# First attention's projections as unrounded half products of 64 stationary columns, in place of three rounded terms

## What is computed

```
x = x + xattn0(queries: context, keys and values: LN(x) and context)
x = x + top-1 of 8 experts, hidden width 512, silu(a) * g
x = x + xattn1(queries: LN(x), 16 heads of 8, keys and values: context)
x = x + top-2 of 8 experts, hidden width 256
```

## Time and profile before

| what | value |
|---|---|
| median of 3 runs | 791.95 us (790.49 to 792.25) |
| span of the profiled execution | 788.3 us |
| what lies between the two | 3.65 us |
| TensorE busy | 706.3 us, 90% |
| its weight loads | 430.8 us, 55% |
| VectorE busy | 475.7 us, 60% |
| ScalarE busy | 378.0 us, 48% |
| GpSimd busy | 377.4 us, 48% |

### The profile page before, as it was taken

One profiled execution on the slowest core, in us unless ns is written; L12 is line 12 of the kernel. 1 busy time (PEld: TensorE's weight loads), 2 busy tenths in 40 slices (PEclk: granted clock), 3 DMA queues, 4 the chain that ended last, 5 costly groups with the idle time before them and its releaser, 6 DMA issues.

```text
span 788.3 us, 13872 instructions
## 1 busy us (share of the span) xinstructions
PE 706.3 (90%) x4810; PEld 430.8 (55%) x4810; DVE 475.7 (60%) x966; ACT 378.0 (48%) x580; POOL 377.4 (48%) x361
## 2 busy tenths in 40 slices
PE   4899999999999999999999999997995687568991
PEld 3654555545556555556545545566995343336661
DVE  4745484585585875667477478465443386845553
ACT  4475554564654554655445444344552643223440
POOL 7264453473464475444464553634333304674552
PEclk9999999999999999999999999998998697569996
DMA  9999999990000000000030004301212500122325
GB/s 253 197 201 197 204 190 10 4 4 1 1 1 2 1 14 1 1 1 1 1 121 2 1 1 108 114 24 32 72 32 80 155 1 28 35 75 69 88 66 177
DMA packets 109867, 50.62 MB, mean 64 GB/s; under 512 B 44804, under 2 KB 103048, under 8 KB 109800
## 3 DMA queue, kind: packets, MB, share of 16 engines
q1 hardware_dynamic: 106280, 42.46, 36.0%
q0 software_dynamic: 3520, 7.27, 2.7%
HBM read 20.07 MB, written 29.64 MB: 63 GB/s over the span
## 4 chain that ended last, share of the span: by engine, by line
PE 74%; DVE 11%; issue 5%; ACT 3%; POOL 3%; DMA 2%; another core or an unknown queue 1%; SPq 1%; DVEq 0%; POOLq 0%; ACTq 0%
PE PSUM L1631 14%; PE PSUM L1663 13%; PE PSUM L1598 5%; PE PSUM L1463 5%; PE PSUM L1498 4%; PE PSUM L1468 4%; PE PSUM L1729 4%; PE PSUM L1423 3%; PE PSUM L1425 2%; PE PSUM L1424 2%; PE PSUM L1612 2%; PE PSUM L1605 2%; PE PSUM L1649 2%; PE PSUM L1693 2%; DVE REC L1377 1%
## 5 line engine op out<-in xcount | busy, mean ns | idle before, releaser
L866 ACT ACTIVATE PT<-PSUM 128x1024 f32<-128x1024 f32 x128 | 128.6, 1024 | 134.1 <-PE PSUM L1631 133.7
L690 POOL TENSOR_TENSOR PSUMS<-PT 128x1024 f32<-128x1024 f32 x32 | 76.0, 2376 | 210.4 <-ACT PT L866 171.4
L690 POOL TENSOR_TENSOR PSUMS<-PSUMS,PT 128x1024 f32<-128x1024 f32 x62 | 149.6, 2413 | 16.8 <-ACT PT L866 9.9
L1254 DVE TENSOR_REDUCE TOPS<-PSUM 128x2 f32<-128x1024 f32 x128 | 152.1, 1220 | 6.9 <-PE PSUM L1598 6.5
L1663 PE MATMUL PSUM<-PT,BIG 128*64 128x512 f32 x512 | 130.6, 611 | 0.0
L1209 DVE TENSOR_TENSOR SIL<-SIL,PSUM 128x256 f32<-128x256 f32 (+1 forms) x62 | 32.2, 519 | 65.7 <-ACT SIL L783 46.8
L1244 DVE TENSOR_TENSOR KL<-PSUM,KH 128x512 fp32r<-128x512 f32 x32 | 22.1, 691 | 68.2 <-ACT KH L844 67.7
L1598 PE MATMUL PSUM<-KH,QH 64*128 64x512 f32 x256 | 57.9, 449 | 4.0 <-DVE QL L1247 3.7
L1663 PEld LDWEIGHTS PSUM<-PT,BIG 128*64 128x64 f32 x512 | 28.4, 135 | 53.4 <-issue 52.0
L1598 PEld LDWEIGHTS PSUM<-KH,QH 64*128 64x128 f32 x256 | 24.2, 183 | 59.2 <-DVE TOPS L1254 24.9
L783 ACT ACTIVATE SIL<-PSUM 128x256 f32<-128x256 f32 (+1 forms) x62 | 28.6, 462 | 56.7 <-PE PSUM L1463 31.4
(11 more groups left out here) (256 smaller groups left out, 1365.5 us busy)
## 6 DMA issues: line engine op xcount, KB each, us to landing
lists_d<-EMPTY SPq DMA_DIRECT2D x3, 2730.0 KB, 35.3
lists_b<-EMPTY SPq DMA_DIRECT2D x3, 2470.0 KB, 33.4
lists_d<-EMPTY SPq DMA_DIRECT2D x1, 2665.0 KB, 34.9
XG<-lists_d SPq DMA_DIRECT2D x39, 65.0 KB
lists_b<-EMPTY SPq DMA_DIRECT2D x1, 2405.0 KB, 17.2
BIG<-in_L_ffn_w SPq DMA_DIRECT2D x1, 2048.0 KB
W2ALL<-in_L_ffn_w SPq DMA_DIRECT2D x4, 512.0 KB, 6.2
PT<-results_d SPq DMA_DIRECT2D x8, 256.0 KB, 4.4
```

Of the source, the lines that this page charges most:

```text
L690: pool.tensor_tensor(PSUMS[:, i % 2], PTT[:, i % 2, 0] if kt == 1 else PSUMS[:, i % 2], PTT[:, i % 2, kt], ALU.add).then_inc(s_ps, 1)
L866: act.activation(PTT[:, i % 2, kt], PSUM[:, place:place + 2, :], ACT.Exp, scale=DH ** -0.5).then_inc(s_exp, 1)
L1254: dve.tensor_reduce(TOPS[:, c, 0, :], PSUM[:, place:place + 2, :], AX.X, ALU.max).then_inc(s_max, 1)
```

## The change

A helper `halves` makes a product as two matmuls of 64 stationary columns, onto partitions 0 to 63 and 64 to 127, with the same moving operand. The projections of the first attention use it on unrounded weights and features instead of `three`. The splits of weights, context and features go, with their buffers (WH, WL, XTH, XTL, CTH, CTL) and semaphores; WA gets a place of its own, and VectorE writes the features straight into XF, two deep. The context values are made once. `qk` has a semaphore for the queries and one for the keys. All other unrounded products named above take the same form, except the down products, gate and up of the second experts, attention × values, and the small sums. The loads of the first experts' gate weights are cut differently: experts 3 and 7 come last.

```diff
-            WH = sb1("WH", 3, INNER)
-            WL = sb1("WL", 3, INNER)
-            XTH = sb1("XTH", 2, S)
-            XTL = sb1("XTL", 2, S)
+            WA = sb1("WA", 3, INNER)
+            XF = sb1("XF", 2, S)
...
             sp.wait_ge(s_sc, context_of(2 * B - 1))
-            gates_of(0, E - 1)
+            gates_of(0, GROUP - 1)
+            gates_of(GROUP, E - 1)
             sp.wait_ge(s_sc, len(scored))
+            gates_of(GROUP - 1, GROUP)
             gates_of(E - 1, E)
...
-                    act.wait_ge(ld_w1, 48)
+                    act.wait_ge(ld_w1, 80)
...
-                    act.wait_ge(s_qk, a + 1)
+                    act.wait_ge(s_qp, a + 1)
...
                     act.activation(QH[:, a % 2, :], PSUM[:, place, :], ACT.Copy).then_inc(s_qkh, 1)
+                    act.wait_ge(s_kp, a + 1)
                     act.activation(KH[:, a % 2, :], PSUM[:, place + 1, :], ACT.Copy).then_inc(s_qkh, 1)
...
-                dve.tensor_scalar(XT[:, :], PSUM[:, bank, :], GAINS[:, 0:1], GAINS[:, 1:2], ALU.mult, ALU.add).then_inc(XTD.sem, 1)
-            def split_features(b):
-                k = b % 2
-                dve.wait_ge(s_xth, b + 1)
-                dve.wait_ge(*XTD.at(b, "feat"))
-                dve.tensor_tensor(XTL[:, k, :], XT[:, :], XTH[:, k, :].bitcast(F32), ALU.subtract).then_inc(XTD.sem, 1)
+                if b >= 2:
+                    dve.wait_ge(s_kp, (b - 1) * PAIRS)
+                    dve.wait_ge(s_vp, (b - 1) * KT)
+                dve.tensor_scalar(XF[:, b % 2, :], PSUM[:, bank, :], GAINS[:, 0:1], GAINS[:, 1:2], ALU.mult, ALU.add).then_inc(s_xf, 1)
...
+            def halves(dst, stationary, moving, start=True, stop=True):
+                for n in range(0, P, 64):
+                    last = pe.matmul(dst[n:n + 64], stationary[:, n:n + 64], moving, start=start, stop=stop)
+                return last
...
-                        last = pe.matmul(PSUM[:, bank + n, c:c + P], WS[:, 2 * (g % 2) + n, c:c + P], XGT[:, g % 3, :],
-                                         start=True, stop=True)
+                        last = halves(PSUM[:, bank + n, c:c + P], WS[:, 2 * (g % 2) + n, c:c + P], XGT[:, g % 3, :])
...
                     for n in range(2):
-                        c = slice(n * BANK, (n + 1) * BANK)
-                        last = three(PSUM[:, place + n, :], XTH[:, k, cols], XTL[:, k, cols], WH[:, 2, c], WL[:, 2, c])
+                        last = halves(PSUM[:, place + n, :], XF[:, k, cols], WA[:, 2, n * BANK:(n + 1) * BANK])
...
-                    for w in range(2):
-                        last = three(PSUM[:, place + w, :], WH[:, w, c], WL[:, w, c], XTH[:, k, :], XTL[:, k, :])
-                    last.then_inc(s_qk, 1)
+                    for w, made in enumerate((s_qp, s_kp)):
+                        halves(PSUM[:, place + w, :], WA[:, w, c], XF[:, k, :]).then_inc(made, 1)
...
-                            last = pe.matmul(PSUM[:, place, t * P:(t + 1) * P], OT[:, (GROUP * a + c) % OTS, t * P:(t + 1) * P],
-                                             WOUT[:, (GROUP * a + c) % PAIRS, :], start=c == 0, stop=c == GROUP - 1)
+                            last = halves(PSUM[:, place, t * P:(t + 1) * P], OT[:, (GROUP * a + c) % OTS, t * P:(t + 1) * P],
+                                          WOUT[:, (GROUP * a + c) % PAIRS, :], start=c == 0, stop=c == GROUP - 1)
...
-                            last = pe.matmul(PSUM[:, c, t * P:(t + 1) * P], QT[a][r, t * P:(t + 1) * P], KBD[r, a, :, :],
-                                             start=True, stop=True)
+                            last = halves(PSUM[:, c, t * P:(t + 1) * P], QT[a][r, t * P:(t + 1) * P], KBD[r, a, :, :])
```

More of the change, by code:

```diff
@@ L259, in build @@
         s_tr = sem("lane_turned")
[L260 to L264, removed]
+        CTD = Steps(sem("ctx_dve"), ["ct", "raw"])
+        s_xf = sem("features")
         s_const_r = sem("rounded_consts")
@@ L1537, in context_keys @@
                     c = slice(pr * P, (pr + 1) * P)
-                    last = three(PSUM[:, 7 - part, pr % GROUP * P:(pr % GROUP + 1) * P], WH[:, 1, c], WL[:, 1, c], CTH[:, :], CTL[:, :])
+                    last = halves(PSUM[:, 7 - part, pr % GROUP * P:(pr % GROUP + 1) * P], WA[:, 1, c], CT)
                 last.then_inc(s_kc, 1)
                 free[7 - part] = s_kcf, part + 1
-            pe.wait_ge(s_cth, 1)
-            pe.wait_ge(*CTD.at(0, "low"))
-            pe.wait_ge(s_wl, 1)
+            pe.wait_ge(*CTD.at(0, "ct"))
+            pe.wait_ge(ld_wk, 16)
             context_keys(0)
-            turn_nrm(RUN_OF["a", 0], 6, XTD.at(0, "feat"))
+            turn_nrm(RUN_OF["a", 0], 6, (s_xf, 1))
             for name, a, place, banks in order_a:
@@ L1568, in tensor_program @@
                         ctx_b = slice(b * M, (b + 1) * M)
-                        for step, weights in enumerate((WH, WL)):
-                            for p in range(GROUP):
-                                last = pe.matmul(
-                                    PSUM[p * M:(p + 1) * M, place + b // 2, b % 2 * 2 * P:(b % 2 + 1) * 2 * P].rearrange("p (g n) -> p g n", g=2),
-                                    CT[:, ctx_b], weights[:, 2, :].bitcast(F32).rearrange("p (g q n) -> p g q n", g=2, q=GROUP)[:, :, p, :],
-                                    start=step == 0, stop=step == 1)
+                        for p in range(GROUP):
+                            last = pe.matmul(
+                                PSUM[p * M:(p + 1) * M, place + b // 2, b % 2 * 2 * P:(b % 2 + 1) * 2 * P].rearrange("p (g n) -> p g n", g=2),
+                                CT[:, ctx_b], WA[:, 2, :].rearrange("p (g q n) -> p g q n", g=2, q=GROUP)[:, :, p, :],
+                                start=True, stop=True)
                     last.then_inc(s_vctx, 1)
@@ L1812, in tensor_program @@
                             r = slice(32 * c, 32 * c + 32)
-                            last = pe.matmul(PSUM[:, c, :], (KBD[r, a, :, :], MINUSC[r, :])[step], (QT[a][r, :], TOPROWC[r, :])[step],
-                                             start=step == 0, stop=step == 1)
+                            last = halves(PSUM[:, c, :], (KBD[r, a, :, :].rearrange("p h k -> p (h k)"), MINUSC[r, :])[step],
+                                          (QT[a][r, :], TOPROWC[r, :])[step], start=step == 0, stop=step == 1)
                     last.then_inc(CPP[a].sem, 1)
@@ L1831, in tensor_program @@
                     for t in range(TPB):
-                        last = pe.matmul(PSUM[:, 7, t * P:(t + 1) * P], OC[:, a % 2, t * P:(t + 1) * P], WC[:, 1, :],
-                                         start=True, stop=True)
+                        last = halves(PSUM[:, 7, t * P:(t + 1) * P], OC[:, a % 2, t * P:(t + 1) * P], WC[:, 1, :])
                     last.then_inc(CPP[a].sem, 1)
@@ L1843, in tensor_program @@
                     for t in range(TPB):
-                        last = pe.matmul(PSUM[:, 7, t * E:(t + 1) * E], FEAT[a][:, t * P:(t + 1) * P], RW[:, 1, :],
-                                         start=True, stop=True)
+                        last = halves(PSUM[:, 7, t * E:(t + 1) * E], FEAT[a][:, t * P:(t + 1) * P], RW[:, 1, :])
                     last.then_inc(RP1[a].sem, 1)
```

91 lines of the change are left out of this document (22 added, 69 removed).

## The result

The changed kernel took 812.67 us (median of 4 runs, 807.84 to 816.59), the kernel before 792.1 us beside it (790.49 to 793.02): **2.5% slower, ratio 1.0247 with an interval of 1.0199 to 1.0295**. The forecast was 813.3 us. The profiled execution is the slowest of the four, 816.59 us with a span of 814.8 us. In a later session the same two kernels lie only 1.4% apart, and that turned out to be the key to which parts of the sum were right. First the rows that answer to those of before.

What follows compares the result with a forecast made beforehand. TensorE was taken to bound the kernel, nearly always busy in the first attention and first experts' tile loop. Terms summed to +21.3 us; with the 788.3 us span and 3.65 us to the median, 813.3 us, range 801 to 824.

Steps and rivals of the forecast that it cites:

- Rivals 1 and 2: Rival 1: pairs at half the price, 741 us, chance 0.11. Rival 2: halves take turns, some 955 us, 0.02.
- Rival 3: Absorbed: projections' additions disappear in waits, edges cost nothing, the start gives more; time within 0.2%; chance 0.03.
- rival 4: Dearer edges: c_top bound by issue, every trip 0.36 us, colder clock; +33 us or more, above 824; chance 0.03.
- 14.6 - 1.3 - 0.4 - 1.8: First attention's projections +14.6 us, waits for QL absorbing 1.3, earlier start -0.4, context values made once -1.8.
- The number of changes of shape stays.: First attention's projections: shape change moves from behind the queries to ahead of them, so only 90 x 0.1625 us is added.
- All that the rounding of the weights did ... was hidden; nothing more is to be had from it.: Start: weight rounding lies ahead of NRM's release at 10.23, so removing it gains nothing; first "top" 1.1 us earlier.
- Outputs +1.9: Output projections, 8 blocks: passes cost the same, shape changes against transposes ahead (0.14 us) and behind (0.25 us) add 1.9.
- Absorbed -1.3: Four second "top" steps wait 0.74 us for QL; that wait swallows the projections' extra 0.33 us each.
- the logits: First attention: the logits stand between two blocks that now have the same shape, so they cost nothing.
- Context values -1.8: Context values drop the second of two steps, 64 passes become 32, half of 3.66 us: -1.8 us.
- Gates +6.3: Gate and up of first experts: passes unchanged, each tile becomes a shape trip, 21 x 0.30 us.
- Second attention +2.0: Second attention and second router: shape trips 1.8 us, c_top's doubled records 0.2 us; upper bound 8 us.

Runs made afterwards that it cites:

- experiment 2: Changed kernel with the first attention's queries, keys and values as whole unrounded products of 128 stationary columns, the rest as halves: 814.66 us, ratio 1.0249.
- gates_only: Kernel before with only gate and up of the first experts as halves: 789.68 us, ratio 1.0087.
- early_again: Same kernel as early_unrounded, run again in the third session: 779.1 us, ratio 0.9973.
- early_unrounded: Kernel before with context keys, first pair's queries and keys, and context values as single whole unrounded products, nothing in halves: 778.7 us, ratio 0.9963.
- early_busy: early_unrounded with six filling matmuls instead of three ahead of the last group's spread: 779.68 us, ratio 0.9984.
- proj_only: Changed kernel with gates, outputs, both routers' logits and second attention whole again; only first attention's projections and context keys as halves: 800.75 us, ratio 1.0083.
- after_third: Changed kernel, unaltered, run again in the third session: 792.27 us, ratio 1.014.
- after_again: Changed kernel, unaltered, run again in the first session of experiments: 813.39 us, ratio 1.024.
- gates_whole: Changed kernel with gate and up of the first experts as whole products again: 803.06 us, ratio 1.0108.

## Why the prediction was right, and where it was right for a wrong reason

**The direction and the mechanism.** A pair costs 0.87 us where three terms cost 0.70; the halves are side by side, each as long as the whole. Rivals 1 and 2 are out by the timeline; rival 1 needed pairs under 0.73. Rival 3 came true in small part (edges that were gains, a start that gave more), and rival 4 not: a tile's edges cost 0.26 us and not 0.36.

**The size.** Up to the last score product the terms of the sum give 14.6 - 1.3 - 0.4 - 1.8 and 7 of the 8 output blocks, 1.7: +12.8 us. Measured: 508.15 to 514.53, +6.4 (514.70 and 514.90 in the other two profiles). Compared iteration by iteration, from one block of turned maxima to the next, `before` and `after` say which steps failed. Where the projections follow the transposes and nothing else comes in, the price of the sum holds: eight iterations with queries and keys alone grew by 0.31 to 0.36 us (0.33 in the sum), four that have values too by 0.67 to 0.69 (0.65).
- *"The number of changes of shape stays."* It does where the projections follow the transposes of the maxima. In 14 of the 31 iterations they follow context scores or sums, and there two changes became one (experiment 2). Three with context sums and values grew by 0.41 to 0.42 us and not by 0.65. Over the ten of the 14 that have no wait (outputs taken off) 2.2 us are missing; the other four are in the last step below.
- *"All that the rounding of the weights did ... was hidden; nothing more is to be had from it."* The features came 1.7 us earlier, 11.40 against 13.09, and the first "top" 2.6 us earlier instead of 1.1. The rows of before, all engines, and then those of `gates_only`, which keeps the rounding:

```profile
7.19 1.22 DVE L988 TENSOR_TENSOR WL<-PT,WH 128x1024 fp32r<-128x1024 f32 x1
7.27 2.04 POOL L649 TENSOR_TENSOR RSTD<-RSTD,MINUS_HALF 128x4 f32<-128x4 f32 x1
...
8.91 1.23 DVE L988 TENSOR_TENSOR WL<-PT,WH 128x1024 fp32r<-128x1024 f32 x1 [0.31 <-ACT WH L759]
9.39 0.80 POOL L651 TENSOR_TENSOR NMR<-NMR,RSTD 128x4 f32<-128x4 f32 x1
```

```profile
9.12 1.23 DVE L988 TENSOR_TENSOR WL<-PT,WH 128x1024 fp32r<-128x1024 f32 x1 [0.55 <-ACT WH L759]
...
9.37 1.04 POOL L651 TENSOR_TENSOR NMR<-NMR,RSTD 128x4 f32<-128x4 f32 x1
```

  GpSimd's two steps of the norm take 2.04 and 0.80 us beside VectorE's subtractions of the rounded weights, and 1.05 and 0.20 where these are gone. In all three profiles of the changed kernel ScalarE's step behind them begins at 8.54 to 8.57, against 10.23 before. The five kernels that keep the subtractions show that these are the cause: the second one starts at 8.70 us (`early_again`), 8.91, 9.01 (`early_unrounded`), 9.12 and 9.28 (`early_busy`), GpSimd's second step takes 0.61, 0.80, 0.84, 1.04 and 1.29 us, and it ends 0.05 or 0.06 us behind the subtraction in all five. I had read the wait for NMR as GpSimd's own pace, without asking what had slowed it. Behind the first "top", TensorE's waits up to the context values shrank as well: in all the start gave 2.3 us more than the sum has for it. The Trainium skill (SBUF — State Buffer, "SBUF: two separate sides") states that a VectorE instruction with two inputs in SBUF and a GpSimd instruction that reads SBUF take turns at one pair of ports; the trace agrees for GpSimd, with this 1.6 us, while VectorE's subtractions took 1.21 to 1.23 us in all of these kernels.
- *Outputs +1.9.* The edges are there, but smaller than I charged. The last transpose ahead of a block is followed after 0.20 us instead of 0.11, and where transposes stand behind the block they add 0.13. Iterations of the changed kernel with an output block are 0.05 to 0.11 us longer than in `proj_only`, where the outputs are whole, and 0.22 with transposes behind: 0.8 us over seven blocks instead of 1.7. The eighth, from the last score to the first gate, shows nothing (`after_third` 17.84 us, `early_again` 17.97).
- *Absorbed -1.3.* The four iterations grew by nothing, -0.03 to +0.01 us, as the sum has it, but not because the wait swallows all 0.33 us. It shrank only from 0.74 to 0.63:

```profile
163.87 0.50 PE L1538 MATMUL PSUM<-KH,QH 64*128 64x512 f32 x2 [0.63 <-DVE QL L1196]
```

  4 x 0.11 = 0.45. These iterations have context sums, so that the projections grew little for the reason of the first step, and the saved edge is the rest of it.

Two smaller things the sum had not seen. The iterations from 449.5 and 478.0 us, for which it has the full 0.33 us each, didn't grow (-0.04 and -0.01): 0.7 us are missing, part of them in waits, one of 0.26 us for ScalarE's exponentials that is gone and one of 0.68 us for QL that is 0.52. And of the logits I had said "nothing"; in two other iterations that have them 0.4 us are missing. Together: 2.2 + 2.3 + 0.9 + 0.7 + 0.4 = 6.5 of the 6.4 us by which that part was too dear.

**The rest of the sum.** Context values -1.8: -1.73, right (35.37 to 37.24 in `early_unrounded` too). Gates +6.3: 4.2 in the loop as put, 7.2 alone in `gates_only`, right. Second attention +2.0: nothing that the later sessions can tell; in the first, its stretch is 86.0 to 89.2 us in the four profiles with halves there and 81.9 and 82.4 in the two without, waits without a named releaser included. A block of 64 small records took 1.50 us there (648.15 to 649.65), 0.4 more than the 32 of the earlier trace rows, where I gave 0.2. By the Trainium skill (TensorE: Matmul & The Clock Gate, "Back-to-back issue gap", on the issue floor) the estimate for it was 1.6 us; that was nearer to the measured 1.50 than my 1.3.

**So the change's own cost is about 12 us, not 21.** In the third session the measurement says 1.014, 11.3 us (the interval reaches from 6 to 16), and its stretches agree: `after_third` less `early_again` is 14.4 us, of which 2.5 is what `early_again` gains itself (39.71 to 37.18).

**What filled the gap in the first session** was in no term. TensorE there waits for ScalarE and VectorE, and these for something that the profile calls remote. Timeline of ACT in `after_again`, then at the same two instructions in `after_third`:

```profile
559.55 0.60 ACT L769 ACTIVATE SIL<-PSUM 128x512 f32<-128x512 f32 x1 [9.03 <-remote]
...
684.96 0.60 ACT L904 ACTIVATE OT<-PSUM 128x512 f32<-128x512 f32 x1 [10.96 <-remote]
```

```profile
553.43 0.60 ACT L769 ACTIVATE SIL<-PSUM 128x512 f32<-128x512 f32 x1 [5.76 <-PE PSUM L1369]
...
673.42 0.60 ACT L904 ACTIVATE OT<-PSUM 128x512 f32<-128x512 f32 x1 [3.97 <-PE PSUM L1363]
```

In the first, the products that ScalarE reads at 559.55 were done by 554.4, and those for 684.96 by 677.3: 5.2 and 7.6 us lost. In `after_third` it starts when they are done, and none of the eight profiles of the later sessions has such a wait, on any engine. The profile of before, with a time like the first session's, has five of ScalarE, 0.84 to 5.96 us long, from 661 to 712 us, none in the first experts. The waits are the 3.0 us by which the way between two early tiles is longer than in the third session (7.22 before, 11.58 and 11.60 after, 8.57 in the third), and part of the 4.5 us and more in the second attention. Where they fall follows the form of the program: `gates_whole` has none in the first experts, and `proj_only` one of 3.6 us there, on VectorE. That the length of the program is the reason is an idea that no run tested. What ScalarE waits for, no run shows.

Another 1.6 us is the clock. The stretch from the last score to the first gate, columns of the earlier trace rows, in `after_again` and in `after_third`:

```profile
514.53:535.09 20.56, 18.96 (x145) 10.00 (x142) 13.80 (x32) 6.58 (x8) 7.65 (x15) 0.92 0.19 55
```

```profile
514.90:532.74 17.84, 17.04 (x144) 8.90 (x141) 13.69 (x32) 6.57 (x8) 7.85 (x15) 1.00 0.22 64
```

The end of the same stretches, timeline of PE:

```profile
528.84 1.89 PE L1376 MATMUL PSUM<-SPREAD,MINUS 128*128 128x512 f32 x4
530.66 4.59 PE L1369 MATMUL PSUM<-WOUT,OT 128*64 128x128 f32 x64
```

```profile
528.06 1.20 PE L1376 MATMUL PSUM<-SPREAD,MINUS 128*128 128x512 f32 x4
529.19 3.71 PE L1369 MATMUL PSUM<-WOUT,OT 128*64 128x128 f32 x64
```

In the first, TensorE was at its lower level of 1.2 GHz for some 3.4 us, over idle products (the first row) and the first part of the last output block (the second), after waits of 0.75, 0.56 and 0.29 us in a stretch at the upper one; from these idle products to the first gate product it took 6.25 us against 4.68. In `after_third` it waited 0.44 and 0.36 us there and stayed at the upper level. Most of the rest of the 2.7 us between the two stretches lies in those waits. So, in the first session: own cost 12 us, waits and clock some 8, together the 20 us between the medians (12 and 12 between the spans of the two profiled executions). The parts of the 8 weren't taken back one by one, and which session is the usual state of a chip isn't known. The forecast met the time by luck: what it had priced too dear, 21 instead of 12 us, and what it had not priced were of a size.

## What to carry to other kernels

Price a product in another form by pitch from start to start, and then count the changes of shape at every kind of neighbour, not at the commonest one: here a block that took its neighbour's shape saved an edge of some 0.2 us, and one that stood alone paid two, 0.26 us. Before calling an engine's work hidden, compare the durations of the same instruction on the other engines beside it and away from it. And where a sum fits but a stretch doesn't, compare stretch by stretch: an experiment is to be set against a run of the changed kernel in its own session.

## What the runs showed of the hardware that was not expected

- One kernel differs between sessions: the kernel before took 793.4 us against 780.9 and 782.5. By the table nearly all of it lies behind the first experts, where the engines wait for each other (9 us), and none in the long stretch (468.44 against 468.24 us).
- Waits of 9 to 11 us of ScalarE that no queue or engine of the profile releases, at the same instructions in three profiles of one session, and none in the others.
- A 4-column operation of GpSimd took 2.04 us beside a 1,024-column VectorE subtraction and 1.05 us away from it, and the next one, 0.20 us by itself, ended with the second subtraction, whenever that one started.
- With 8 moving columns (the first router's logits) the passes of two halves followed each other after 0.059 us a pair, where whole passes took 0.112: the three blocks of logits in the long stretch take 2.08 us against 2.44 from their first start to the next product, less 0.09 us that each costs more at the edge ahead of it. There alone the pairs gained.
